# Second layer's attention output: turned probabilities as weights, values of one head moving

## What is computed

```python
xn = layer_norm(x, norm_w, norm_b)
q = (xn @ q_w + q_b).reshape(Bx, Tx, H, -1)      # H = 16 heads of 32
k = (xn @ k_w + k_b).reshape(Bx, Tx, H, -1)
att = jnp.einsum('bnhl,bmhl->bnmh', q, k)
att = jax.nn.softmax(att + (1.0 - mask) * -1000000.0, axis=2)
v = ((xn @ v_w + v_b) * src_mask[:, :, None]).reshape(Bx, Tx, H, -1)
y = jnp.einsum('bnmh,bmhl->bnhl', att, v).reshape(Bx, Tx, Dx)
h = layer_norm(y, sb_norm_w, sb_norm_b) * (1.0 + scale) + shift
return x + jax.nn.silu(h) @ out_w + out_b
```

## Time and profile before

| what | us |
|---|---|
| median of 3 runs | 2022.38 (2020.29 to 2022.92) |
| the profiled execution, its own time | 2023.43 |
| span of the profile | 2021.5 |
| PE busy | 1994.3 (99%) |
| VectorE busy | 1383.8 (68%) |
| ScalarE busy | 1152.8 (57%) |
| GpSimd busy | 596.3 (29%) |

### The profile page before, as it was taken

One profiled execution on the slowest core, in us unless ns is written; L12 is line 12 of the kernel. 1 busy time (PEld: TensorE's weight loads), 2 busy tenths in 40 slices (PEclk: granted clock), 3 DMA queues, 4 the chain that ended last, 5 costly groups with the idle time before them and its releaser, 6 DMA issues.

```text
span 2021.5 us, 52452 instructions
## 1 busy us (share of the span) xinstructions
PE 1994.3 (99%) x19377; PEld 1722.5 (85%) x19377; DVE 1383.8 (68%) x3505; ACT 1152.8 (57%) x3806; POOL 596.3 (29%) x985
## 2 busy tenths in 40 slices
PE   7999999999999999999999999999999999999998
PEld 5888888888888888888888888888888888888886
DVE  6777777777777777776666666656565666666665
ACT  4333443334433344344777777777777777777775
POOL 3333333333333333335122222222222222222220
PEclk9999999999999999999999999999999999999999
DMA  6311111111111111113101010101010101011000
GB/s 228 118 47 35 40 42 47 47 37 39 42 47 47 37 38 42 47 47 107 39 24 42 21 42 26 37 26 37 26 37 26 37 26 37 30 33 42 21 32 22
DMA packets 54856, 90.55 MB, mean 45 GB/s; under 512 B 4333, under 2 KB 17257, under 8 KB 54825
## 3 DMA queue, kind: packets, MB, share of 16 engines
q1 hardware_dynamic: 54640, 90.06, 13.2%
q10 hardware_dynamic: 184, 0.07, 0.0%
HBM read 56.46 MB, written 33.65 MB: 45 GB/s over the span
## 4 chain that ended last, share of the span: by engine, by line
PE 95%; DVE 2%; ACT 1%; DMA 0%; issue 0%; POOL 0%; ACTq 0%; SPq 0%; POOLq 0%; DVEq 0%
PE bank L544 16%; PE bank L546 14%; PE bank L545 14%; PE bank L553 10%; PE bank L554 9%; PE bank L555 9%; PE bank L565 7%; PE bank L1831 3%; PE bank L1806 3%; PE bank L1170 3%; PE bank L1156 2%; PE bank L1763 2%; PE bank L1800 1%; PE bank L1065 1%; PE bank L1841 1%; ACT heads L1618 1%
## 5 line engine op out<-in xcount | busy, mean ns | idle before, releaser
L553 PE MATMUL bank<-xT_hi,w_hi 128*128 128x256 f32 x1536 | 449.6, 293 | 0.7 <-DVE v L524 0.6
L554 PE MATMUL bank<-xT_lo,w_hi 128*128 128x256 f32 x1536 | 439.3, 286 | 0.0
L555 PE MATMUL bank<-xT_hi,w_lo 128*128 128x256 f32 x1536 | 436.5, 284 | 0.0
L1618 ACT ACTIVATE heads<-bank,top 128x128 f32<-128x128 f32 x1024 | 361.0, 405 | 88.0 <-DVE top L1401 87.9
L979 ACT ACTIVATE heads<-heads,k_neg 128x128 f32<-128x128 f32 x256 | 79.3, 391 | 447.3 <-POOL k_neg L719 447.3
L544 PE MATMUL bank<-w_hi,xT_hi 128*128 128x512 f32 x768 | 307.6, 401 | 4.1 <-DVE bias_all L390 4.1
L553 PEld LDWEIGHTS bank<-xT_hi,w_hi 128*128 128x128 f32 x1536 | 293.5, 191 | 11.1 <-issue 4.6
L546 PE MATMUL bank<-w_lo,xT_hi 128*128 128x512 f32 x768 | 301.1, 392 | 0.0
L545 PE MATMUL bank<-w_hi,xT_lo 128*128 128x512 f32 x768 | 300.9, 392 | 0.0
L554 PEld LDWEIGHTS bank<-xT_lo,w_hi 128*128 128x128 f32 x1536 | 293.9, 191 | 0.2 <-issue 0.2
L555 PEld LDWEIGHTS bank<-xT_hi,w_lo 128*128 128x128 f32 x1536 | 293.7, 191 | 0.0
(11 more groups left out here) (202 smaller groups left out, 3739.9 us busy)
## 6 DMA issues: line engine op xcount, KB each, us to landing
xr<-in_x SPq DMA_DIRECT2D x32, 512.0 KB, 3.5
x_between_layers<-ends SPq DMA_DIRECT2D x64, 256.0 KB, 2.0
xr<-x_between_layers SPq DMA_DIRECT2D x32, 512.0 KB, 4.1
out<-ends SPq DMA_DIRECT2D x64, 256.0 KB, 2.1
key_mask<-mask_parts SPq DMA_DIRECT2D x32, 128.0 KB, 3.3
store<-in_L_cond_W_emb SPq DMA_DIRECT2D x4, 1024.0 KB, 10.5
store<-in_L_cond_emb_w SPq DMA_DIRECT2D x3, 1024.0 KB, 8.2
mask_rows<-mask_parts SPq DMA_DIRECT2D x128, 2.0 KB
```

The source lines that it names most:

```text
L553: yield nc.tensor.matmul(dst, w_hi[:, m, c, fs], a_hi[:, c], start=(first and c == 0), stop=False)
L554: yield nc.tensor.matmul(dst, w_hi[:, m, c, fs], a_lo[:, c], start=False, stop=False)
L555: yield nc.tensor.matmul(dst, w_lo[:, m, c, fs], a_hi[:, c], start=False, stop=(last and c == C - 1))
L1618: last = nc.scalar.activation(prob[:, a, c, :], ps[a][:, c * P:(c + 1) * P], ACT.Exp, bias=top[:, b, h:h + 1], accum_out=total[:, b, h:h + 1])
```

## The change

`mixed` swaps its operands: for each head the turned probabilities (128 keys x 128 queries) are the weights, over the whole array, and the values of the head (128 keys x 32) move through them. y then comes out by rows, each head into 32 columns of the same bank. `turned`, `copy_yT`, the tile `yT` and two semaphores go; `mixed` tells VectorE itself that y is there. Where the transposes were woven into other matmuls, these now run alone. Nothing else is changed, and the code that waits for `y_ps` on VectorE is the same. Cut to its core:

```diff
@@ scalar
-        def copy_yT(prev, b, bank=None):
-            bank = Y_BANKS[b] if bank is None else bank
-            act.wait_ge(s["yT_ps"], seq(PAIR, prev, b + 1))
-            nc.scalar.activation(yT[:], ps[bank][:, :].rearrange("p (c t) -> p c t", c=C),
-                                 ACT.Copy).then_inc(s["yT"], 1)
...
         def step1(i):
-            copy_yT(i, 0)
             exps(i, 1)
@@ tensor, mixed
             for c in range(C):
                 for a in range(HC):
-                    last = nc.tensor.matmul(ps[bank][DH * a:DH * a + DH, c * P:(c + 1) * P],
-                                            v[:, b, HC * c + a, :], prob_T[:, a, c, :], start=True, stop=True,
-                                            tile_position=(0, DH * a))
-            last.then_inc(s["yT_ps"], 1)
-
-        def turned(prev, b, bank=None):
-
-            bank = Y_BANKS[b] if bank is None else bank
-            pe.wait_ge(s["yT"], seq(PAIR, prev, b + 1))
-            for c in range(C):
-                last = nc.tensor.transpose(ps[bank][:, c * P:(c + 1) * P], yT[:, c, :], ident[:])
-                if c == C - 1:
-                    last.then_inc(s["y_ps"], 1)
-                yield
+                    h = HC * c + a
+                    last = nc.tensor.matmul(ps[bank][:, h * DH:(h + 1) * DH], prob_T[:, a, c, :], v[:, b, h, :],
+                                            start=True, stop=True)
+            last.then_inc(s["y_ps"], 1)
@@ tensor, step0
             scores(i, 0)
-            woven(out_rows(i - 1, 0), turned(i - 1, 1))
+            run(out_rows(i - 1, 0))
             run(value_rows(i, 0))
@@ tensor, step1
-            woven(projected(i + 1, K, (0, 1)), turned(i, 0))
+            run(projected(i + 1, K, (0, 1)))
             run(projected(i + 1, K, (2, 3)))
@@ tensor, last_pair
             outputs = out_rows(LAST - 1, 1, OTHER_O_BANK)
-            run(islice(outputs, 2))
-            woven(turned(LAST, 0, LAST_Y_BANKS[0]), islice(outputs, C))
+            run(islice(outputs, 2 * C))
             mixed(LAST, 1, LAST_Y_BANKS[1])
-            run(islice(outputs, 3))
-            woven(turned(LAST, 1, LAST_Y_BANKS[1]), outputs)
+            run(outputs)
```

More of the change, by code:

```diff
@@ L151, in build @@
             "x_biased", "qk_ps", "k", "q", "masks_in", "v_ps", "v", "s_ps", "top", "prob", "pT_ps", "pT",
-            "yT_ps", "yT", "y_ps", "p_sum", "y", "y_stats", "y_var", "y_var_eps", "y_rstd", "z", "z_ps",
+            "y_ps", "p_sum", "y", "y_stats", "y_var", "y_var_eps", "y_rstd", "z", "z_ps",
             "gains", "g", "tanh", "silu", "h_hi", "h_lo", "o_ps", "out", "g_last", "stored0", "stored1", "raw0", "raw1", "raw2", "raw3",
@@ L1204, in layer1 @@
     v = m.v1[:].rearrange("p (b h d) -> p b h d", b=PAIR, h=H)
-    yT = sb("yT", [P, C, P])
     prob = m.heads[:, 0:H * P].rearrange("p (a c t) -> p a c t", a=HC, c=C)
@@ L1697, in step0 @@
         def step0(i, first):
-            if not first:
-                copy_yT(i - 1, 1)
             exps(i, 0)
@@ L1730, in scalar @@
         loop(act, NP, body)
-        copy_yT(LAST - 1, 1)
         exps(LAST, 0)
@@ L1737, in scalar @@
         exps(LAST, 1, (1, 2, 3), True)
-        copy_yT(LAST, 0, LAST_Y_BANKS[0])
         last_prob_out((0, 1))
-        copy_yT(LAST, 1, LAST_Y_BANKS[1])
         gate(LAST, 0, LAST_Z_BANKS[0])
@@ L1945, in last_pair @@
             scores(LAST, 0)
-            woven(out_rows(LAST - 1, 0), turned(LAST - 1, 1))
+            run(out_rows(LAST - 1, 0))
             run(value_rows(LAST, 0))
```

## The result

The changed kernel takes 2240.93 us (median of 4 runs, 2234.36 to 2244.2) where the kernel before takes 2022.39: a ratio of 1.108, with a 95% interval of 1.1063 to 1.1096. It is slower, as forecast, but outside the range of 2150 to 2195.

A forecast was written before the change was run, and what follows sets the result against it. TensorE at 2.4 GHz was taken as the bound, beside a fixed exps chain: 62 x 2.46 + 2.9 = 155.4 us on the profiled 2023.43 gave 2178.8, with the median 1.05 lower 2178 us; range 2150 to 2195.

The forecast's parts named there:

- What bounds the kernel now: Second layer: TensorE, 99% busy at 2.4 GHz; each step a fixed stretch from scores to last exp, then one TensorE fills.
- Mixed: Changed product: 32 weight loads at 0.1115 us set the pace, 3.56 us for 1.10, +2.46 us a call.
- The rival of loads and stream that don't overlap: In mixed, the 32 columns add 0.83 us a call, 53 in all: 2231; no or partial overlap, chance 0.10.
- The sum at a full clock: Whole kernel: 62 calls of mixed at +2.46 us plus 2.9 for the last pair, 155.4 us more.
- The transposes at nothing: Removing yT's four transposes (0.44 us a call) before the wait for the exps gains 0, as TensorE waits instead.
- The bound that was left: Most that the removed yT transposes could gain in step 1, through its near tie with the exps: 1.6 us in all.
- The first rival: Removed yT transposes count in one step (2164) or in both (2151); range 2151 to 2169, chance 0.10.
- The copy at nothing: Removing ScalarE's copy of yT (64 x 0.6 us) gains 0: it ends before the first maximum arrives.
- The last pair: Final two calls of mixed and the unchanged chain behind them: +2.9 us, copy and transposes already set off.
- The third rival: In mixed, the stream and not the load sets the pace, a call takes 1.0 us: 2016, chance 0.02.
- What the profile after would show: 128x128 loads in mixed, a pair grown by 4.9 us, yT lines gone, waits for the exps 0.4 us longer.

The follow-up runs named there:

- fillers: The changed kernel with 64 moving columns in mixed, plus four transposes of the unit matrix per step where those of yT stood: 2179.4 us, ratio 1.0782.
- the gaps filled: The changed kernel, still with 32 moving columns, plus four transposes of the unit matrix per step where those of yT stood: 2244.87 us, ratio 1.1108.

## Why the prediction was wrong

**What bounds the kernel now**: right up to the clock. The step that failed is the sentence that took the granted clock of the earlier trace rows as given ("which is the 2.4 GHz level. So a microsecond of PE work in the second layer costs a microsecond") and made the sum at that level alone. What the clock could cost was put at nothing without a reason. No rival had the clock in it, though the change turned 1.01 us of four column tiles at work into 3.58 us of loads. In its place the runs show a fall to 1.2 GHz at or behind 35 of 62 calls, worth 2240.9 - 2177.9 = 63 us against the kernel with 64 columns.

**Mixed**: right. 30 paces of 0.1115 and an exit of 0.21 gave 3.56 us a call, measured 3.58. The row with one moving column was the right neighbour, though it couldn't tell whether 32 columns stay hidden: the one-column row, 32, 64 and 128 columns all keep a pace of 0.11. The rival of loads and stream that don't overlap falls with that, though 2241 lies near its 2231: that is chance, the passes of the changed kernel stand 0.112 us apart. The sum at a full clock, 2022.4 + 155.4 = 2177.8, is what the 64-column kernel measured: 2177.87. So near a match is partly luck, since the runs beside that kernel had a before of 2021.31, and its own four span 5 us.

**The transposes at nothing**: right, shown twice, at the old mixed (2021.06 for 2021.31) and at the new one (2177.87 without, 2179.4 with fillers). The two kinds of step without them are 0.05 to 0.06 us shorter each than before (16.24 and 16.67 against 16.29 and 16.73). The bound that was left, "0.05 us a step 1", thus holds for step 1, and as much goes in step 0, where nothing was left; together some 3 us of the 28, no more than the medians can tell. The first rival (2151 to 2164) falls.

**The copy at nothing**: shown together with the transposes, not apart from them.

**The last pair**: +2.9 was forecast. There the clock fell, too, and the changed kernel's tail says nothing. At 64 columns the whole span grew by 2174.9 - 2021.5 = 153.4, against a sum of 155.4, which leaves little room for an error in it.

**The third rival**, faster by a stream-bound pace: no sign of it.

**What the profile after would show**: the load shape, the lost lines and the longer wait in steps with a full clock were as written. A pair grew by 4.9 us only where the clock was full in both steps.

What stays open: why the clock falls at some calls and not at others. The falls come again in a pattern (one or two of 6.83 us, then two of 3.41, with steps at a full clock between them), but no run here takes apart what sets it. Nor is it shown what about the surplus columns keeps the clock up. The Trainium skill's page "TensorE: Matmul & The Clock Gate", in its section "The HAM clock gate (the 'warmup' mystery)", says that the clock follows how busy PE has been, and its advice in "Why this matters for your kernels" is to leave no idle gaps between bursts of matmuls. In this case the trace differs in one point: PE had no idle gap in the profile with the gaps filled (700.00 us busy of 700.00), and the clock still fell, at or behind the stretches that are mostly loads. The fillers are transposes, and no run here shows whether those weigh as much for the clock as products do.

## What to carry to other kernels

Before swapping operands, price a matmul by the larger of its stream and the next weight load: a moving side of 32 under 128 columns of 4-byte weights costs 0.11 us a pass, as much as 128 columns would. Then ask what the array streams during the new stretch; here 3.6 us of mostly loads cost another 3% through the clock, and moving 64 or 128 columns in place of 32, which cost nothing under the loads, gave that back. And before crediting a removed step on a "99% busy" engine, look for a wait behind it that another engine ends: its distance from that engine's last instruction stays the same from pair to pair.

## What the runs showed that was not expected

- The granted clock fell to the 1.2 GHz level 35 times while PE was busy throughout, 2.8 to 4.7 us after the start of a call of 3.58 us in which each load of 128 columns met 32 moving ones. With 64 or 128 moving columns it never fell in this layer ahead of the last pair, with the call just as long; with 32 and a call of 1.80 us neither.
- A kernel that moves four times the columns through the array in mixed is 61 us faster (2179.6 against 2240.9).
- A product of 512 columns (0.234 us from one to the next) hides one weight load of 0.11 us, not two: 0.68 us for four small passes and one product, woven or not.
